# Last attention of a four-layer transformer kernel: VectorE takes over a quarter of GpSimd's subtractions of the row maximum

## The chip, the cores and the metric

One Trainium2 chip, one core. The metric is the device time of one execution in microseconds, as the median of several runs. The engines are named as in the profile: PE is TensorE (PEld its weight loads), DVE is VectorE, ACT is ScalarE, POOL is GpSimd, SP is SyncE, which issues DMAs.

## The reference, cut to what matters

Four layers, each an attention and a feed-forward block, on x of 16 sequences x 128 positions x 256 features. Everything is float32 unless a block quantizes. The change touches only the attention of the last layer:

```python
scores = jnp.einsum('bhqd,bhkd->bhqk', q, k) / np.sqrt(D)      # 32 heads of 8, keys of two windows
scores = scores + bias[None]                                   # ALiBi slopes
scores = jnp.where(mask[None, None], scores, -jnp.inf)         # 64 back for one half, 32 for the other
wei = jax.nn.softmax(scores, axis=-1)
return jnp.einsum('bhqk,bhkd->bhqd', wei, v)
```

## The kernel before, in words

The stage is `window_attention`. The work runs over 16 batches (one sequence of 128 positions each), written as pairs: `t` counts pairs and `j` is 0 or 1 in a pair. This text numbers the batches 0 to 15. Each batch has eight units (`U`), in two quads of four (`QUAD`). A unit is a 128 x 512 tile: four blocks of 128 rows (head and query) by 128 keys.

For each unit, four engines follow one another:

- PE computes the scores of a whole quad into four PSUM banks (`scores`, L3171). The first quad of a batch needs the queries spread by GpSimd (`made`) and the keys copied by ACT (`keyed`); each quad needs the four banks read by VectorE (`biased`).
- VectorE's `lower` (L3325): four instructions per unit add the table of slopes and mask to the scores, write the sum to `low` in SBUF and reduce the row maximum into `top`. One operand of each comes from PSUM, one from SBUF. The last of the four counts up `biased`.
- GpSimd's `lower` (L3141): one 128 x 512 instruction per unit subtracts `top` from `low` in place; both operands lie in SBUF. It counts up `lowered`.
- PE transposes the unit (`turn_probs`, L3180), ACT takes the exponential (L3274), and later PE multiplies by the values (`mix_up`, L3197).

GpSimd also spreads the queries of the next batch, in two instructions of 128 x 512 (`spread`, L2884). Its order in a batch is: lower of units 0 and 1, spread 0, lower of units 2 and 3, spread 1, lower of units 4 to 7.

VectorE's order in a batch is: `lower` of units 4 to 7; `normalize` of the second quad of the batch before (a reciprocal, L3336, and a product, L3338); `add` of the batch two back (x += result, L3344, and the statistics of the row, L3346); `lower` of units 0 to 3 of the next batch; `normalize` of this batch's first quad. Batch 1 has no `add` yet, batch 0 neither.

PE's order in a batch is written out by hand: transposes of units 0 and 1, scores of this batch's second quad, half of the batch before's product with the values, transpose of unit 2, `turn_mixed`, transpose of unit 3, `turn_back`, `go_down` (output projection of the batch two back), transposes of units 4 and 5, scores of the next batch's first quad, first half of this batch's product, transposes of units 6 and 7, `turn_back`. Each engine runs its queue in order, and a waiting instruction holds all that stands behind it.

Ahead of the last pair (batches 14 and 15) VectorE works out the variance of the first 12 row blocks (L2056 to L2061) and GpSimd its inverse root (`norm.root`, L2065), which stands on GpSimd's queue ahead of the subtractions of batch 14; `norm.shifts` (L2069) follows on VectorE in batch 15. SP moves values and results through HBM by DMA (`read_values`, `realign`), in step with `normalize`.

Of the kernel before, what the change touches and what calls it, by code (L numbers as in the profile page):

```python
# [9 lines left out]
ALU = mybir.AluOpType  # L10
# [4 lines left out]
P = 128  # L15
# [2864 lines left out]
def spread_queries(pool, w, c, queries, place):  # L2880

    query = queries.rearrange("p (i q) -> p i q", q=QB).unsqueeze(2).to_broadcast([P, NB, 4, QB])
    own = w.own[:, :].unsqueeze(1).unsqueeze(3).to_broadcast([P, NB, 4, QB])
    return pool.tensor_tensor(w.qd[:, place, :, c * (P // 2):(c + 1) * (P // 2)].rearrange("p i (m q) -> p i m q", q=QB), query, own, ALU.mult)  # L2884
# [186 lines left out]
def window_attention(nc, mem, norm):  # L3071


    U = NB
    QUAD = 4
    LOWS = 8
# [4 lines left out]
    with ctx:  # L3081
        def sb(what, shape, dt=F32):
            return ctx.enter_context(nc.sbuf_tensor(f"wa_{what}", shape, dt))
# [4 lines left out]
        def signal(what, per=1, credit=0):  # L3088
            return Signal(ctx, nc, f"wa_{what}", 2 * per, credit)
# [3 lines left out]
        low = mem.ctxt[:, :, :].rearrange("p c (l x n) -> p (c l) x n", l=LOWS // HC, x=QUAD)  # L3093
        pt = sb("pt", [P, U // 2, QUAD, 2, P])
        top = sb("top", [P, LOWS, QUAD])
# [13 lines left out]
        v_read = [Signal(ctx, nc, f"wa_v_read{j}", 32) for j in range(2)]  # L3109
        scored = signal("scored", U, 2 * U)  # L3110
        biased = signal("biased", U, 2)
        lowered = signal("lowered", U)
        turn = signal("turn", U, LOWS)
        pt_moved = signal("pt_moved", U, 2)
        mixed_s = signal("mixed", U // 2, U)
# [11 lines left out]
        with nc.Block() as block:  # L3127

            @block.gpsimd
            def _(pool):  # L3130
                pool.memset(v[:, :, :, WV:], 0.0).then_inc(padded.sem, 1)

                def spread(t, j, c):
                    if c == 0:
                        pool.wait_ge(scored.sem, scored.at(t, (j - 2) * U + U - 1))
                    spread_queries(pool, w, c, w.q[:, c, bass.ds((t * 2 + j) * S, S)], j % 2).then_inc(made.sem, 1)

                def lower(t, j, k):
                    pool.wait_ge(biased.sem, biased.at(t, j * U + k))
                    unit = low[:, k % LOWS, :, :]  # L3140
                    pool.tensor_tensor(unit, unit, top[:, k % LOWS, :].unsqueeze(2).to_broadcast([P, QUAD, P]), ALU.subtract).then_inc(lowered.sem, 1)  # L3141

                def batch(t, j, final=False):
                    for k in range(U):
                        lower(t, j, k)
                        if k in (1, 3) and not final:
                            spread(t, j + 1, k // 2)

                pool.sem_inc(made.sem, HC)
                for t in range(B // 2 - 1):  # L3150
                    batch(t, 0)
                    batch(t, 1)
                norm.root(pool, 0, 0, LASTG)
                batch(B // 2 - 1, 0)
                batch(B // 2 - 1, 1, final=True)

            @block.tensor
            def _(pe):
# [15 lines left out]
                                last.then_inc(scored.sem, 1)  # L3174

                def turn_probs(t, j, k):
                    pe.wait_ge(lowered.sem, lowered.at(t, j * U + k))
                    pe.wait_ge(pt_moved.sem, pt_moved.at(t, j * U + k - 2))
                    for x in range(QUAD):
                        last = pe.transpose(turned[k % 2][:, x * P:(x + 1) * P], low[:, k % LOWS, x, :], mem.ident[:, :])  # L3180
                    last.then_inc(turn.sem, 1)
# [68 lines left out]
                t = B // 2 - 1  # L3250
# [63 lines left out]
            @block.vector  # L3314
            def _(dve):
                for s in (biased, chain, added):
                    dve.sem_inc(s.sem, s.credit)

                def lower(t, j, k):
                    n = j * U + k  # L3320
                    unit = low[:, k % LOWS, :, :]
                    dve.wait_ge(scored.sem, scored.at(t, n))
                    dve.wait_ge(turn.sem, turn.at(t, n - LOWS))
                    for x in range(QUAD):
                        ins = dve.tensor_tensor_reduce(unit[:, x, :], score[k % QUAD][:, x * P:(x + 1) * P], w.table[:, k, x, :], 1.0, NEVER,  # L3325
                                                       ALU.add, ALU.max, top[:, k % LOWS, x:x + 1])
                    ins.then_inc(biased.sem, 1)

                def normalize(t, j, u):
                    def step(k, ins):  # L3330
                        ins.then_inc(chain.sem, 1)
                        dve.wait_ge(chain.sem, chain.at(t, 4 * j + 2 * u + k))

                    sums = back[:, :].rearrange("p (x k d) -> p x k d", x=QUAD, k=4)
                    dve.wait_ge(backed.sem, backed.at(t, 2 * j + u))
                    step(0, dve.reciprocal(inv[:, :, :], sums[:, :, :, WD]))  # L3336
                    dve.wait_ge(placed[u].sem, placed[u].at(t, 16 * j - 1))
                    step(1, dve.tensor_tensor(mixed[:, u, :, :].rearrange("p x (k d) -> p x k d", k=4), sums[:, :, :, 0:WD],  # L3338
                                              inv[:, :, :].unsqueeze(3).to_broadcast([P, QUAD, 4, WD]), ALU.mult))

                def add(t, j):
                    row = mem.x_tile(t * 2 + j)
                    dve.wait_ge(downed.sem, downed.at(t, j))
                    dve.tensor_tensor(row, row, od[:, H:2 * H], ALU.add).then_inc(added.sem, 1)  # L3344
                    dve.wait_ge(added.sem, added.at(t, j))
                    dve.bn_stats(mem.stats_tile(t * 2 + j), row).then_inc(stat.sem, 1)  # L3346

                def batch(t, j, before=2, final=False):
                    if final:
                        norm.shifts(dve, 0, 0, LASTG)  # L3350
                    for k in range(QUAD, U):
                        lower(t, j, k)
                    if before >= 1:
                        normalize(t, j - 1, 1)
                    if before >= 2:
                        add(t, j - 2)
                    if not final:
                        for k in range(QUAD):
                            lower(t, j + 1, k)
                    normalize(t, j, 0)  # L3360
                    if final:
                        norm.scales(dve, 0)
                        norm.lift(dve, 0)

                for k in range(QUAD):
                    lower(0, 0, k)
                batch(0, 0, before=0)
                batch(0, 1, before=1)
                for t in range(1, B // 2 - 1):
                    batch(t, 0)  # L3370
                    batch(t, 1)
                t = B // 2 - 1
                dve.wait_ge(stat.sem, stat.at(t, -3))
                norm.variance(dve, 0, LASTG)
                batch(t, 0)
                batch(t, 1, final=True)
                norm.round(dve, 0)
                normalize(t, 1, 1)
                add(t, 0)

# [420 lines left out]
def layer3_attention(nc, mem, A, norm):  # L3801
    ctx = Stage(nc)
    with ctx:
        def sb(name, shape, dt=F32):
            return ctx.enter_context(nc.sbuf_tensor(f"wa_{name}", shape, dt))

        w = mem.wa
        w.q = sb("q", [P, HC, T])
        w.kc, w.ko = sb("kc", [P, W_CTX + T]), sb("ko", [P, W_OWN + T])
        w.qd, w.keys = sb("qd", [P, 2, NB, P]), sb("keys", [P, 2, NB, P])  # L3810
        window_projections(nc, mem, mem.norm_projections)
        window_attention(nc, mem, norm)
# [273 lines left out]
```

## Time and profile before

| what | value |
|---|---|
| median of 3 runs | 2010.26 us (2015.07, 2008.82, 2010.26) |
| the profiled execution, its own time | 2015.13 us |
| its span, first to last instruction | 2013.4 us |
| mean granted TensorE clock | 0.963 of full speed |
| stage of the change, first scores to last statistics | 1703.5 to 1893.5 us of the span |

How to read it: the profiled execution is one run, 0.24% above the median; 1.7 us of it lie around the span. A timeline gives start and length in us, and in brackets the idle time of the engine before the instruction and what ended it; neighbours of one kind are merged, with their count behind an x. Pipelined instructions may overlap.

### The profile page before, as it was taken

What the parts mean: (1) busy time and instruction counts of PE and PEld (TensorE: products, weight loads), DVE (VectorE), ACT (ScalarE), POOL (GpSimd) and SP (SyncE); (2) the same over time, 40 slices, a digit from 0 to 9 for tenths busy, and PEclk for the clock granted to TensorE, in tenths of its full rate; (3) what the DMA queues carried; (4) which work ended last, traced back from release to release, by engine and by line L of the source; (5) the groups of instructions that cost most, each with busy time, mean ns of one, the idle gap of its engine ahead of it and who ended that gap; (6) DMA issues with size and microseconds to landing.
All of it is one profiled execution on the core that took longest, in us unless ns stands there. A gap on an engine that the chain in (4) does not pass through costs nothing. (4 is left out here: it accounts for less than half of the span.)

```text
span 2013.4 us, 42500 instructions
## 1 busy us (share of the span) xinstructions
PE 1792.1 (89%) x12207; PEld 1211.7 (60%) x12216; DVE 1264.2 (63%) x4137; ACT 1026.1 (51%) x2698; POOL 729.0 (36%) x707
## 2 busy tenths in 40 slices
PE   7999999998999888859899999987997879999765
PEld 4677777775555556645566666663554555787533
DVE  5666666664777534565543344446997954787697
ACT  5555555554333344411344444435887942666586
POOL 3333333332000100557455555552320011998420
PEclk9999999999999999979999999998998889999888
DMA  9990000000000000135577777650001021222100
GB/s 311 304 274 0 0 0 0 0 0 1 0 0 0 1 1 1 70 135 176 142 164 161 164 162 171 117 123 1 2 2 66 1 70 41 43 54 58 36 22 22
DMA packets 145607, 145.55 MB, mean 72 GB/s; under 512 B 49376, under 2 KB 133568, under 8 KB 145344
## 3 DMA queue, kind: packets, MB, share of 16 engines
q1 hardware_dynamic: 122432, 113.81, 19.5%
q0 software_dynamic: 23040, 30.01, 8.5%
q8 instruction: 75, 1.23, 0.3%
q14 instruction: 60, 0.49, 0.1%
HBM read 137.12 MB, written 66.44 MB: 101 GB/s over the span
## 5 line engine op out<-in xcount | busy, mean ns | idle before, releaser
L1709 POOL DMA_INDIRECT expert_sums<-moe_rows_in,moe_to x128 | 198.2, 1549 | 159.2 <-DMA expert_sums<-moe_rows_in,moe_to 101.6
L1782 PE MATMUL moe_gate<-moe_places,moe_xt 128*128 x512 | 175.9, 466 | 4.2 <-issue 2.0
L1975 DVE COPY moe_ht_e<-moe_turned 128x256 f32<-128x256 f32 x128 | 54.3, 424 | 194.4 <-PE moe_turned L1790 194.4
L570 ACT ACTIVATE ga_prob<-ga_score,ga_neg_max 128x128 f32<-128x128 f32 x256 | 99.6, 390 | 125.7 <-DVE ga_neg_max L443 125.7
L2065 POOL TENSOR_TENSOR ln_rstd<-ln_var,half 128x4 f32<-128x4 f32 (+1 forms) x16 | 21.4, 1338 | 367.2 <-DVE ln_var L2061 367.2
L190 POOL TENSOR_TENSOR ga_q_inv<-ga_q_sum,half 128x4 f32<-128x4 f32 x64 | 64.4, 1007 | 224.4 <-DVE ga_q_sum L426 224.4
L3325 DVE CUSTOM_DVE_ANT_0 ctxt<-wa_score,early 128x128 f32<-128x128 f32 x512 | 110.8, 287 | 46.9 <-PE wa_score L3171 46.9
L3141 POOL TENSOR_TENSOR ctxt<-ctxt,wa_top 128x512 f32<-128x512 f32 x128 | 129.8, 1040 | 17.1 <-DVE wa_top L3325 17.1
L325 PE MATMUL ga_summed<-ga_wo,ga_out_t 128*128 128x256 f32 x512 | 121.2, 380 | 0.7 <-ACT ga_out_t L578 0.7
L1782 PEld LDWEIGHTS moe_gate<-moe_places,moe_xt 128*128 128x128 f32 x512 | 90.8, 190 | 48.6 <-issue 13.6
L249 PE MATMUL ga_proj<-early,ga_xt 128*128 128x512 f32 x252 | 119.8, 598 | 0.0
L1116 POOL DMA_INDIRECT slot_x<-early x96 | 98.6, 1027 | 54.1 <-issue 27.1
L439 DVE SCALAR_TENSOR_TENSOR ga_score<-ga_scored,ga_q_inv,ga_mask 128x128 f32<-128x128 f32 x256 | 72.2, 344 | 51.6 <-PE ga_scored L297 51.2
L325 PEld LDWEIGHTS ga_summed<-ga_wo,ga_out_t 128*128 128x128 f32 x512 | 92.3, 190 | 11.0 <-ACT ga_out_t L578 1.1
L1889 ACT ACTIVATE moe_act_e<-moe_gate 128x176 f32<-128x176 f32 x128 | 40.6, 317 | 101.6 <-PE moe_gate L1782 101.6
L3180 PE MATMUL wa_turned<-ident,ctxt 128*128 128x128 f32 x512 | 77.3, 286 | 11.3 <-POOL ctxt L3141 10.0
L3274 ACT ACTIVATE wa_pt<-wa_turned 128x512 f32<-128x512 f32 x128 | 73.1, 596 | 25.8 <-PE wa_turned L3180 23.3
L431 DVE COPY ga_qt<-ga_turned 128x512 f32<-128x512 f32 x63 | 43.4, 689 | 62.6 <-PE ga_turned L289 62.5
L297 PEld LDWEIGHTS ga_scored<-ga_kt,ga_qt 128*128 128x128 f32 x512 | 63.7, 192 | 23.6 <-DVE ga_qt L431 13.9
L556 ACT ACTIVATE ga_square<-ga_q_tok 128x128 f32<-128x128 f32 x256 | 75.0, 294 | 1.5 <-DVE ga_q_tok L394 1.4
L297 PE MATMUL ga_scored<-ga_kt,ga_qt 128*128 128x128 f32 x512 | 72.5, 285 | 0.9 <-DVE ga_qt L431 0.9
L1884 ACT ACTIVATE moe_xt<-moe_up 128x256 f32<-128x256 f32 x128 | 49.2, 384 | 47.0 <-PE moe_up L1771 36.5
(491 smaller groups left out, 4700.2 us busy)
## 6 DMA issues: line engine op xcount, KB each, us to landing
moe_places<-in_L_ffn_packed SPq DMA_DIRECT2D x128, 608.0 KB
slot_x<-zeros SPq DMA_DIRECT2D x24, 1076.0 KB, 14.8
moe_rows_in<-slot_x SPq DMA_DIRECT2D x128, 134.5 KB, 3.2
wa_v<-v_ctx SPq DMA_DIRECT2D x16, 180.0 KB, 3.2
early<-in_L_xattn_Wq SPq DMA_DIRECT2D x5, 512.0 KB, 7.8
x<-in_x SPq DMA_DIRECT2D x4, 512.0 KB, 9.6
ga_wo<-in_L_xattn_Wo SPq DMA_DIRECT2D x1, 2048.0 KB, 15.0
expert_sums<-zeros SPq DMA_DIRECT2D x2, 1024.0 KB, 7.9
```

The costliest lines, as they stand in the source:

```text
L249: last = pe.matmul(proj[m % 2][:, :], lhs[:, c, :], weight[:, c, :], start=(c == 0), stop=(c == HC - 1))
L297: last = pe.matmul(scored[n % 2][:, h * P:(h + 1) * P], qt[:, n % 2, h * P:(h + 1) * P], kt[:, b % 2, g, :], start=True, stop=True)
L325: last = pe.matmul(summed[:, 0:H], out_t[:, h, :], w.wo[:, h, :], start=(h == 0), stop=(h == NH - 1))
L556: last = act.activation(square[:, h, :], q_tok[:, n % 2, h * D:(h + 1) * D], ACT.Square, accum_out=q_sum[:, n % 2, h:h + 1])
L570: last = act.activation(prob[:, n % 2, part], score[:, n % 2, part], ACT.Exp, bias=neg_max[:, n % 2, h:h + 1], accum_out=total[:, n % 2, h ...
L1116: pool.indirect_dma_start(out=self.mem.slot_x, out_offset=bass.IndirectOffsetOnAxis(ap=self.slot_to[:, t, k:k + 1], axis=0), in_=self.mem. ...
L1709: pool.indirect_dma_start(out=mem.sums[j % SUMS], out_offset=bass.IndirectOffsetOnAxis(ap=to[:, j:j + 1], axis=0), in_=y[:, j, :], in_offs ...
L1782: last = pe.matmul(both[j % 2][:, 0:2 * FE], xt[:, j % 2, c, :], packed[:, place, c * 2 * FE:(c + 1) * 2 * FE].rearrange("p a n -> p (a n) ...
L3141: pool.tensor_tensor(unit, unit, top[:, k % LOWS, :].unsqueeze(2).to_broadcast([P, QUAD, P]), ALU.subtract).then_inc(lowered.sem, 1)
L3180: last = pe.transpose(turned[k % 2][:, x * P:(x + 1) * P], low[:, k % LOWS, x, :], mem.ident[:, :])
L3274: act.activation(pt[:, k // 2, :, k % 2, :], turned[k % 2][:, :].rearrange("p (x m) -> p x m", x=QUAD), ACT.Exp).then_inc(pt_moved.sem, 1)
L3325: ins = dve.tensor_tensor_reduce(unit[:, x, :], score[k % QUAD][:, x * P:(x + 1) * P], w.table[:, k, x, :], 1.0, NEVER, ALU.add, ALU.max, ...
```

## The change

VectorE subtracts the maximum of units 3 and 7 itself, after `lower` of the quad that they end, and waits for its own `biased` first; a semaphore `lowered_v` tells PE. GpSimd subtracts for units 0, 1, 2, 4, 5, 6. The second spread is tied to unit 2 and no longer to unit 3.

```diff
-        lowered = signal("lowered", U)
+        lowered = signal("lowered", U - 2)
+        lowered_v = signal("lowered_v", 2)
...
                 def batch(t, j, final=False):
                     for k in range(U):
-                        lower(t, j, k)
-                        if k in (1, 3) and not final:
-                            spread(t, j + 1, k // 2)
+                        if k % QUAD < QUAD - 1:
+                            lower(t, j, k)
+                        if k in (1, 2) and not final:
+                            spread(t, j + 1, k - 1)
...
                 def turn_probs(t, j, k):
-                    pe.wait_ge(lowered.sem, lowered.at(t, j * U + k))
+                    u, r = divmod(k, QUAD)
+                    if r == QUAD - 1:
+                        pe.wait_ge(lowered_v.sem, lowered_v.at(t, j * 2 + u))
+                    else:
+                        pe.wait_ge(lowered.sem, lowered.at(t, j * (U - 2) + u * (QUAD - 1) + r))
...
+                def subtract(t, j, u):
+                    k = QUAD * u + QUAD - 1
+                    unit = low[:, k % LOWS, :, :]
+                    dve.wait_ge(biased.sem, biased.at(t, j * U + k))
+                    dve.tensor_tensor(unit, unit, top[:, k % LOWS, :].unsqueeze(2).to_broadcast([P, QUAD, P]), ALU.subtract).then_inc(lowered_v.sem, 1)
...
                     for k in range(QUAD, U):
                         lower(t, j, k)
+                    subtract(t, j, 1)
                     if before >= 1:
                         normalize(t, j - 1, 1)
...
                         for k in range(QUAD):
                             lower(t, j + 1, k)
+                        subtract(t, j + 1, 0)
                     normalize(t, j, 0)
...
                 for k in range(QUAD):
                     lower(0, 0, k)
+                subtract(0, 0, 0)
```

## Rows read from the trace of the kernel before

**Rows 1.** The page, busy time, share of the span and instructions of each engine.
```profile
PE 1792.1 (89%) x12207; PEld 1211.7 (60%) x12216; DVE 1264.2 (63%) x4137; ACT 1026.1 (51%) x2698; POOL 729.0 (36%) x707
```

**Rows 2.** Stretches between the first scores of consecutive batches: busy time of each engine.
```profile
core 0: us, PE busy (x) PEld busy (x) DVE busy (x) ACT busy (x) POOL busy (x), PEclk, DMA share, GB/s
1725.54:1736.50 10.96, 10.55 (x239) 9.03 (x238) 8.52 (x70) 6.96 (x13) 10.01 (x11) 1.00 0.26 54
...
1845.22:1856.10 10.88, 10.56 (x240) 9.04 (x239) 8.71 (x71) 7.11 (x14) 10.03 (x11) 1.00 0.26 54
1856.10:1874.27 18.17, 12.17 (x239) 10.37 (x238) 9.47 (x77) 7.06 (x14) 13.36 (x13) 0.81 0.16 33
```

**Rows 3.** Waits from 1735 to 1873 us: total, times, longest (us).
```profile
PEld wa_turned L3180 <- POOL ctxt L3141: 9.6, 12, 6.0
```

**Rows 4.** Timeline of GpSimd in one batch.
```profile
1771.34 2.04 POOL L3141 TENSOR_TENSOR ctxt<-ctxt,wa_top 128x512 f32<-128x512 f32 x2 [0.85 <-DVE wa_top L3325]
1773.33 1.04 POOL L2884 TENSOR_TENSOR wa_qd<-wa_q,early 128x512 f32<-128x512 f32 x1
...
1777.33 4.04 POOL L3141 TENSOR_TENSOR ctxt<-ctxt,wa_top 128x512 f32<-128x512 f32 x4
```

**Rows 5.** Timeline of PE in the same batch.
```profile
1771.27 1.09 PE L3180 MATMUL wa_turned<-ident,ctxt 128*128 128x128 f32 x8
...
1774.02 1.17 PE L3171 MATMUL wa_score<-wa_keys,wa_qd 32*128 32x128 f32 x32
...
1779.01 1.06 PE L3180 MATMUL wa_turned<-ident,ctxt 128*128 128x128 f32 x8
1780.01 1.17 PE L3171 MATMUL wa_score<-wa_keys,wa_qd 32*128 32x128 f32 x32
```

**Rows 6.** Timeline of VectorE around the same batch's first half.
```profile
1767.81 0.26 DVE L3336 RECIPROCAL wa_inv<-wa_back 128x16 f32<-128x16 f32 x1
...
1768.42 0.42 DVE L3344 TENSOR_TENSOR x<-x,wa_mix_t 128x256 f32<-128x256 f32 x1
1768.88 0.43 DVE L3346 BATCH_NORM_STATS2 stats<-x 128x6 f32<-128x256 f32 x1
...
1770.33 0.29 DVE L3325 CUSTOM_DVE_ANT_0 ctxt<-wa_score,early 128x128 f32<-128x128 f32 x1 [1.02 <-PE wa_score L3171]
...
1773.71 0.25 DVE L3336 RECIPROCAL wa_inv<-wa_back 128x16 f32<-128x16 f32 x1
...
1775.30 0.29 DVE L3325 CUSTOM_DVE_ANT_0 ctxt<-wa_score,early 128x128 f32<-128x128 f32 x1 [1.02 <-PE wa_score L3171]
```

**Rows 7.** By line: instructions of these kinds, ns min/median/max.
```profile
L420 DVE TENSOR_TENSOR ga_k_rms<-ga_k_tok,ga_k_inv x16: 681/692/694, 17.0 to 450.1; 128x512 f32<-128x512 f32 x16
...
L3141 POOL TENSOR_TENSOR ctxt<-ctxt,wa_top x128: 1036/1040/1046, 1705.7 to 1884.5; 128x512 f32<-128x512 f32 x128
```

**Rows 8.** Timeline and lines: VectorE and GpSimd, both with two SBUF operands, side by side.
```profile
L2069 DVE SCALAR_TENSOR_TENSOR ln_shift<-ln_mean,ln_rstd x16: 150/158/1074, 452.1 to 1929.1; 128x4 f32<-128x4 f32 x12, 128x12 f32<-128x12 f32 x4
...
1876.48 4.04 POOL L3141 TENSOR_TENSOR ctxt<-ctxt,wa_top 128x512 f32<-128x512 f32 x4 [1.91 <-DVE wa_top L3325]
...
1879.47 1.07 DVE L2069 SCALAR_TENSOR_TENSOR ln_shift<-ln_mean,ln_rstd 128x12 f32<-128x12 f32 x1
...
1880.46 0.28 DVE L3325 CUSTOM_DVE_ANT_0 ctxt<-wa_score,early 128x128 f32<-128x128 f32 x1
...
L2010 DVE TENSOR_TENSOR x<-x,moe_places x8: 406/420/772, 1345.2 to 1360.5; 128x256 f32<-128x256 f32 x8
...
L1718 POOL TENSOR_TENSOR x<-x,moe_places x8: 715/722/904, 1345.3 to 1358.2; 128x256 f32<-128x256 f32 x8
...
1349.54 1.58 POOL L1718 TENSOR_TENSOR x<-x,moe_places 128x256 f32<-128x256 f32 x2
...
1349.77 0.77 DVE L2010 TENSOR_TENSOR x<-x,moe_places 128x256 f32<-128x256 f32 x1
```

**Rows 9.** Timeline ahead of batch 14: VectorE's end of its lowers, GpSimd's inverse root.
```profile
1860.67 0.26 DVE L3336 RECIPROCAL wa_inv<-wa_back 128x16 f32<-128x16 f32 x1
...
1862.21 2.27 POOL L2065 TENSOR_TENSOR ln_rstd<-ln_var,half 128x12 f32<-128x12 f32 x1 [4.76 <-DVE ln_var L2061]
```

## The prediction

> **What bounds the kernel now.** The page comes first and settles little: PE is busy for 89% of the span, GpSimd for 36% [rows 1], but that averages many stages. So the stage is cut into batches. Twelve stretches, from the first scores of batch 2 to those of batch 14, last 10.87 us each within 0.1, and in each PE is busy for 10.55, GpSimd for 10.0, VectorE for 8.7 [rows 2] (the first and the last of the twelve stand there). Two engines are close to full, and which of them sets the 10.87 has to be read from order and waits, not from shares.
>
> Take VectorE's first `lower` of a batch as zero, D = 1770.33 [rows 6]. GpSimd starts 1.01 later (1771.34) and then issues one instruction per 1.00 us: units 0 and 1, spread 0 (1773.33, D+3.00), and so on, until unit 7 ends at 1777.33 + 4.04 = 1781.37 [rows 4]. PE transposes units 0 and 1 as GpSimd yields them and issues the second quad's scores at 1774.02, D+3.69. From there to the next batch's scores (1780.01, D+9.68) its own list of work fills the time. The test is units 4 and 5, the last subtractions ahead of those scores: their eight transposes take 1.06 us, and those of units 6 and 7, whose subtractions lay ready long before, take 1.09 [rows 5]. So GpSimd delays PE at units 4 and 5 by nothing that shows; it arrives just in time. PE's weight loads do wait for GpSimd, 9.6 us in 12 waits, but 6.0 of that is one wait ahead of batch 14 [rows 3], and what remains, about 0.33 per batch, belongs to units 0 and 1, which the change leaves as they are. VectorE has slack in two places: 1.02 us ahead of each quad's first `lower` [rows 6].
>
> **What the change removes.** Two GpSimd instructions of 1.04 us [rows 7] per batch, 32 in all. Only unit 3 stands ahead of units 4 and 5, which come about 1 us earlier; PE doesn't wait for them, so this is worth 0. Units 0 and 1 follow VectorE, not GpSimd's backlog: GpSimd idles 0.85 ahead of unit 0 already [rows 4]. The cover that makes the removal worthless is PE's own list. Tying the second spread to unit 2 moves nothing: GpSimd's order is units 0, 1, spread 0, unit 2, spread 1, unit 4 either way, once unit 3 is gone.
>
> **What it adds.** Two VectorE subtractions per batch of 128 x 512 with both operands in SBUF. The nearest row of the same kind and size lasts 0.69 us (L420) [rows 7]. If that were all, each would fit into a 1.02 us slack, with the wait on its own `biased` (about 0.11: an estimate for the last accumulator read and the semaphore; between add and statistics such a wait shows 0.04, 1768.84 to 1768.88 [rows 6]). Behind the first subtraction stand `normalize` and the second quad's lowers; behind the second stand `normalize`, `add` and the next batch's lowers, so what overflows the slack reaches D.
>
> **What the two engines do to each other.** In this stage an instruction of 0.158 us on VectorE with two SBUF operands lasted 1.07: it began at 1879.47 and ended at 1880.54, 0.02 behind GpSimd's run of subtractions (1876.48 + 4.04 = 1880.52) [rows 8]. Elsewhere VectorE's sum of 0.42 came upon a GpSimd sum of 0.72 begun at 1349.54 (to 1350.26), and ended at 1350.54: 0.28 behind it, 0.14 short of its full length; the second GpSimd sum then ended at 1351.12, 0.58 behind VectorE, again 0.14 short [rows 8]. So the later one waits out the earlier and keeps a lead of about 0.13, and VectorE gets in between two GpSimd instructions. VectorE's `lower` reads PSUM and escapes: sixteen took 3.38 us beside a busy GpSimd (1770.33 to 1773.71) [rows 6].
>
> Walk through one batch after the change:
> - First subtraction ready at D + 3.38 + 0.11 = D+3.49. GpSimd is in spread 0, from D+3.01 to D+4.05. It ends at F = D + 4.05 + 0.69 - 0.13 = D+4.61.
> - GpSimd's unit 2 ends at F + 1.04 - 0.14 = F+0.90. Unit 4 starts at F+1.86, unit 5 at F+2.86, unit 6 at F+3.86, and that ends at F+4.90.
> - VectorE's next instruction begins 0.08 ahead of the end (1880.46 against 1880.54 [rows 8]); `normalize` takes 0.61 (1767.81 to 1768.42 [rows 6]). Unit 4's `lower` starts at F+0.53, and the second subtraction is ready at F + 0.53 + 3.49 = F+4.02.
> - That is 0.16 behind the start of GpSimd's unit 6. It waits and ends at F + 4.90 + 0.56 = F+5.46.
> - Then `normalize` 0.61, `add` 0.46 (1768.42 to 1768.88), statistics 0.43 less 0.08 [rows 6]: the next D is F + 5.46 - 0.08 + 0.61 + 0.46 + 0.35 = F+6.80 = D+11.41.
>
> PE would allow D+10.87. VectorE becomes the bound, by **0.54 us per batch**. Batches 2 to 13 carry the whole list: 12 x 0.54 = 6.5. Batch 1 has no `add` (0.8 less) and fits. PE's transposes of units 3 and 7 then wait for F and F+5.46; PE comes to them later than that.
>
> Ahead of batch 14 the first subtraction stands between the last `lower` (1860.67) and the variance, behind which GpSimd has idled 4.76 us [rows 9], and PE 6.0 [rows 3]. GpSimd being idle, it costs 0.69 + 0.11 - 0.08 = 0.72, all on the path. In batches 14 and 15 the second subtraction ends ahead of PE's scores or of the tail, so nothing is added. SP's value loads and stores follow `normalize` by some 0.7 to 1.8 us more and have several us of room: 0.
>
> **Sum**: 6.5 + 0.7 = 7.2 us. The profiled execution of 2015.13 would become 2022.3; it lies 0.24% above the median of 2010.26, which becomes **2017.5**.
>
> The Trainium skill, "SBUF — State Buffer", section "Who interferes with whom", says that a VectorE instruction with two SBUF inputs and a GpSimd instruction that reads SBUF exclude each other, and that the second to issue "fully blocks" until the first has ended. The rows agree on the exclusion and differ on the full block, by the lead of 0.13. By the page, F would be D+4.74, the next D F+7.07, the excess 0.94 per batch, and the time 2022.3, with the second subtraction a mere 0.03 behind unit 6.
>
> **The rivals.**
> - *The second subtraction slips ahead of GpSimd's unit 6.* It then ends at F + 3.90 + 0.56 = F+4.46, the next D would be F+5.80 = D+10.41, below PE's 10.87, and only the 0.7 ahead of batch 14 is left: 2011.0, no change. It decides if the subtraction is ready 0.16 us earlier against GpSimd than worked out. For it: the margin is thin, and every term has an error of some hundredths. Against it: at 1879.47 VectorE still lost to a GpSimd instruction of the run that began within hundredths of it [rows 8]. The same time results if a subtraction with a broadcast operand escapes the exclusion. Chance 0.27.
> - *VectorE doesn't get in between GpSimd's instructions and waits until GpSimd idles.* Then F = D + 6.05 + 0.56 = D+6.61, unit 4's `lower` starts at D+7.14, GpSimd's units 4 to 6 end at D+11.20, and the next D is D+13.10: 2.2 x 12 + 0.7, 2037.5. Against it stand the two GpSimd sums at 1349.54 with VectorE's between them [rows 8]. Chance 0.05.
> - *The full block of the page*, 2022.3: 0.04.
> - *GpSimd was the bound after all* and loses an instruction of 1.00 per batch on its loop from unit 0 to unit 5: 13 fewer, 1998. Against it is the 1.06 beside 1.09 [rows 5]. Chance 0.04.
>
> **How the numbers follow.** The forecast above has 0.60; its own range is 2014.5 to 2020.5 (0.54 moves with the subtraction's length by twice 0.07, the runs scatter by several us). Within 0.3% (6.0 us) is about what a measurement of this kernel can't tell from no change. Of the forecast, 0.48 lies above that and 0.12 below. Slower: 0.48 + 0.05 + 0.04 = 0.57. Same: 0.12 + 0.27 = 0.39. Faster: 0.04. The range runs from 2009 (no change, with scatter) to 2022.5 (the full block).
>
> **What would show it.** Stretches between first scores of 11.4 us, with PE's busy time unchanged. VectorE's subtractions of about 1.1 us (the first, ending 0.56 behind spread 0) and 1.4 us (the second, 0.56 behind unit 6), not 0.69; GpSimd's unit 2 about 0.46 longer. No wait of VectorE for scores ahead of a batch, and PE's weight loads waiting more for GpSimd's unit 0. GpSimd's inverse root 0.7 later against the last `lower` of batch 14. Wrong would be: stretches of 10.9 with a second subtraction of 0.7 to 1.0 us (it slipped ahead), or of 9.9 (GpSimd was the bound).

## The result: slower, by the steps forecast, and at a time outside the range

The changed kernel ran 2027.36 us as the median of four runs (2018.74 to 2031.82), the kernel before 2009.65 (the three runs listed above and a fourth, 2009.04); the ratio is 1.0077, interval 1.0045 to 1.0109. The direction was forecast; the time lies 9.9 us above the forecast of 2017.5 and 4.9 above the top of the range. Measured again, twice, with 12 runs of the changed kernel beside 35 of the one before, the ratio is 1.0027 (1.0004 to 1.0051) and 1.0032 (1.0007 to 1.0057), against the forecast 2017.5 / 2010.26 = 1.0036.

The profiled execution after took 2018.74 us (span 2016.9). The page's row of engines, to lay beside [rows 1]:

```profile
PE 1787.8 (89%) x12207; PEld 1212.4 (60%) x12216; DVE 1298.4 (64%) x4169; ACT 1026.5 (51%) x2698; POOL 704.0 (35%) x675
```

VectorE has 32 instructions more, GpSimd 32 fewer. VectorE's sum grew by 34.2 us, where 32 x 0.69 would be 22.1. The stretches from first scores to first scores, one that stands for eleven equal ones and the one ahead of batch 15 (columns as in [rows 2]):

```profile
1764.82:1776.17 11.35, 10.60 (x240) 9.09 (x239) 11.11 (x73) 7.12 (x14) 8.48 (x8) 1.00 0.25 51
1855.62:1875.65 20.03, 12.87 (x240) 10.92 (x239) 12.09 (x82) 7.10 (x14) 10.30 (x9) 0.83 0.14 30
```

10.87 has become 11.35. PE is as busy as before (10.60 beside 10.55), at the same granted clock of 1.00; VectorE is now busy for 11.11 of the 11.35, GpSimd for 8.48 where it was 10.0.

One batch after the change, GpSimd first, then VectorE (its lowers left out but for the first of each quad), then PE:

```profile
1767.52 2.04 POOL L3142 TENSOR_TENSOR ctxt<-ctxt,wa_top 128x512 f32<-128x512 f32 x2 [2.87 <-DVE wa_top L3331]
1769.52 1.04 POOL L2884 TENSOR_TENSOR wa_qd<-wa_q,early 128x512 f32<-128x512 f32 x1
1770.52 1.49 POOL L3142 TENSOR_TENSOR ctxt<-ctxt,wa_top 128x512 f32<-128x512 f32 x1
1771.97 1.04 POOL L2884 TENSOR_TENSOR wa_qd<-wa_q,early 128x512 f32<-128x512 f32 x1
1772.97 3.04 POOL L3142 TENSOR_TENSOR ctxt<-ctxt,wa_top 128x512 f32<-128x512 f32 x3
```

```profile
1765.73 0.42 DVE L3356 TENSOR_TENSOR x<-x,wa_mix_t 128x256 f32<-128x256 f32 x1
1766.19 0.43 DVE L3358 BATCH_NORM_STATS2 stats<-x 128x6 f32<-128x256 f32 x1
1766.53 0.27 DVE L3331 CUSTOM_DVE_ANT_0 ctxt<-wa_score,early 128x128 f32<-128x128 f32 x1
...
1770.02 1.09 DVE L3339 TENSOR_TENSOR ctxt<-ctxt,wa_top 128x512 f32<-128x512 f32 x1
...
1771.64 0.29 DVE L3331 CUSTOM_DVE_ANT_0 ctxt<-wa_score,early 128x128 f32<-128x128 f32 x1
...
1775.14 1.41 DVE L3339 TENSOR_TENSOR ctxt<-ctxt,wa_top 128x512 f32<-128x512 f32 x1
...
1777.88 0.28 DVE L3331 CUSTOM_DVE_ANT_0 ctxt<-wa_score,early 128x128 f32<-128x128 f32 x1
```

```profile
1764.82 1.17 PE L3173 MATMUL wa_score<-wa_keys,wa_qd 32*128 32x128 f32 x32
1766.37 1.10 PE L3203 MATMUL wa_mix_t<-wa_pt,wa_v 128*32 128x64 f32 x64 [0.37 <-issue]
```

The walk of the prediction can be laid over these rows, with D = 1766.53:

| step | forecast | measured |
|---|---|---|
| first subtraction ready | D+3.49 | 1770.02, D+3.49 |
| its length, its end F | 1.1 us, D+4.61 | 1.09, 1771.11, D+4.58 |
| GpSimd's unit 2 ends | F+0.90 | 1770.52 + 1.49 = 1772.01, F+0.90 |
| GpSimd's unit 6 ends | F+4.90 | 1772.97 + 3.04 = 1776.01, F+4.90 |
| second subtraction ready | F+4.02 | 1775.14, F+4.03 |
| its length, its end | 1.4 us, F+5.46 | 1.41, 1776.55, F+5.44 |
| next D | F+6.80, D+11.41 | 1777.88, F+6.77, D+11.35 |

No wait is left between VectorE's instructions: the 1.02 us ahead of each quad [rows 6] are gone, and its list sets the batch. PE shows it as 0.37 us of idle time ahead of its product (L3203). The profile names no releaser for it ("issue"), but in the code the product waits for `added` of the batch two back, and the `add` above ended at 1765.73 + 0.42 = 1766.15, 0.22 before the product.

Then the two ends. Ahead of batch 14 (VectorE, then GpSimd), beside [rows 9]:

```profile
1860.82 0.69 DVE L3339 TENSOR_TENSOR ctxt<-ctxt,wa_top 128x512 f32<-128x512 f32 x1
1861.42 0.25 DVE L3348 RECIPROCAL wa_inv<-wa_back 128x16 f32<-128x16 f32 x1
```

```profile
1862.96 2.27 POOL L2065 TENSOR_TENSOR ln_rstd<-ln_var,half 128x12 f32<-128x12 f32 x1 [7.50 <-DVE ln_var L2061]
```

Here GpSimd is idle, and the same subtraction takes 0.69. In batch 15 (VectorE, then PE):

```profile
1885.84 1.10 DVE L3339 TENSOR_TENSOR ctxt<-ctxt,wa_top 128x512 f32<-128x512 f32 x1
1886.86 0.24 DVE L3348 RECIPROCAL wa_inv<-wa_back 128x16 f32<-128x16 f32 x1
1887.14 0.29 DVE L3350 TENSOR_TENSOR tail_mixed<-wa_back,wa_inv 128x128 f32<-128x128 f32 x1
1887.47 0.42 DVE L3356 TENSOR_TENSOR x<-x,wa_mix_t 128x256 f32<-128x256 f32 x1
```

```profile
1885.67 1.04 PE L3186 MATMUL wa_turned<-ident,ctxt 128*128 128x128 f32 x8
1888.10 1.10 PE L3203 MATMUL wa_mix_t<-wa_pt,wa_v 128*32 128x64 f32 x64 [1.40 <-ACT wa_pt L3280]
```

PE stood for 1.40 us ahead of the product of batch 15. The profile names ScalarE's exponential, but the last exponentials that this product needs are those of units 1 and 3; the `add` of batch 13 ended at 1887.89, 0.21 before the product, the same distance as in the batch above. In the kernel before, the same product follows without a wait, but its `add` had ended only 0.28 us ahead of it (1884.57 + 0.42 = 1884.99), and had itself waited for PE's output projection:

```profile
1884.57 0.42 DVE L3344 TENSOR_TENSOR x<-x,wa_mix_t 128x256 f32<-128x256 f32 x1 [0.15 <-PE wa_mix_t L3218]
```

```profile
1885.26 1.10 PE L3197 MATMUL wa_mix_t<-wa_pt,wa_v 128*32 128x64 f32 x64
```

So in batch 15 there was next to no room for a later `add` before either.

The stage, cut into the same pieces in every kernel (us from first scores to first scores; "within 14" is from first to second scores of batch 14, "last" from the second scores of batch 15 to the start of the last statistics, and "stage" ends there too, 0.43 ahead of the 1893.5 that the table of the kernel before has for their end). The first stretch is 11.11, 11.30 or 12.03 in executions of one and the same kernel, and is longer where the granted clock is lower, so it is none of the change; here batch 0 of before and of after, the clock in the third column from the end:

```profile
1703.57:1714.66 11.09, 8.14 (x88) 6.47 (x88) 6.94 (x64) 3.82 (x7) 8.70 (x9) 0.69 0.47 102
```

```profile
1697.33:1709.35 12.02, 9.35 (x88) 7.42 (x88) 8.22 (x66) 3.57 (x7) 8.16 (x8) 0.58 0.43 95
```

| kernel | batch 0 | batch 1 | mean of 2 to 13 | within 14 | last | stage |
|---|---|---|---|---|---|---|
| before | 11.11 | 10.88 | 10.88 | 11.48 | 13.92 | 189.5 |
| after | 12.03 | 10.33 | 11.33 | 12.71 | 15.38 | 198.6 |
| after, again | 11.11 | 10.32 | 11.32 | 12.71 | 15.49 | 197.1 |
| after, third time | 11.30 | 10.33 | 11.33 | 12.71 | 15.38 | 197.0 |
| reduction in place of subtraction | 11.11 | 9.93 | 10.85 | 12.20 | 14.66 | 189.7 |
| unit 3 alone | 12.03 | 10.32 | 10.86 | 12.21 | 14.00 | 190.7 |
| unit 7 alone | 12.03 | 10.88 | 10.97 | 11.51 | 14.77 | 193.5 |
| unit 7 behind the statistics | 12.03 | 10.32 | 10.85 | 12.21 | 14.26 | 191.0 |
| units 3 and 7 not subtracted | 12.04 | 9.93 | 10.91 | 11.49 | 13.92 | 190.4 |
| unit 7 behind the statistics in batch 15 only | 11.13 | 10.33 | 11.32 | 12.70 | 14.26 | 195.9 |
| before, late inverse root | 12.03 | 10.88 | 10.88 | 4.88 | 14.97 | 185.8 |
| before, late root and late shift | 11.11 | 10.88 | 10.88 | 4.88 | 14.22 | 184.1 |

### The profile page after: what moved, and what is told of

It reads as the page before. It is cut to its first block and busy times, and to the rows that moved or that the text cites. A ratio compares the mean times of both kernels' runs of the same rounds, so it can differ in the third digit from the quotient of the medians.

```text
span 2016.9 us, 42500 instructions
## 1 busy us (share of the span) xinstructions
PE 1787.8 (89%) x12207; PEld 1212.4 (60%) x12216; DVE 1298.4 (64%) x4169; ACT 1026.5 (51%) x2698; POOL 704.0 (35%) x675
## 5 line engine op out<-in xcount | busy, mean ns | idle before, releaser
L3142 POOL TENSOR_TENSOR ctxt<-ctxt,wa_top 128x512 f32<-128x512 f32 x96 | 104.1, 1105 | 47.1 <-DVE wa_top L3331 47.1
L3186 PEld LDWEIGHTS wa_turned<-ident,ctxt 128*128 128x128 f32 x512 | 58.1, 145 | 23.6 <-POOL ctxt L3142 17.1
```

## The experiments

The intervals of most of these ratios overlap, and that of the changed kernel (1.0027, from 1.0004 to 1.0051) too. So it is the stretches and lengths of one profiled execution of each kernel that decide between the theories, not the times.

**The changed kernel once more.** No edit.

> The changed kernel once more, unaltered, to see where the runs some 9 to 13 us above the profiled one (2018.7 against 2027 to 2032) lose their time. Theory 1 (the exclusion alone): the stage is 9 us longer than before in every run (stretches of 11.35 us instead of 10.87), the rest is scatter of other stages, and the median comes out near 2009.6 + 9 = 2018 to 2020. Theory 2 (something else in this stage comes on top in most runs, such as a lower granted clock because PE now idles in each batch): the median stays at 2025 to 2029, and a profile of such a run shows a granted clock of 0.5 inside the stage or stretches above 11.4 us.

Measured: 2019.19 us (2010.13 to 2027.93, 12 runs), the kernel before beside it 2013.39 (2004.18 to 2026.64, 35 runs), ratio 1.0027 (1.0004 to 1.0051). Against the table's first row the stage is 7.6 us longer (the 9 us expected came from the first profile, where batch 0 alone took 0.9 more): -0.6 in batch 1, +5.3 in batches 2 to 13 (scores to scores), +1.2 within batch 14, +1.6 at the end.

**A reduction in place of each subtraction.** VectorE runs as many instructions, of the same 128 x 512, in the same places, but each reads one operand from SBUF; the maximum of units 3 and 7 stays in.

```diff
-                    dve.tensor_tensor(unit, unit, top[:, k % LOWS, :].unsqueeze(2).to_broadcast([P, QUAD, P]), ALU.subtract).then_inc(lowered_v.sem, 1)
+                    dve.tensor_reduce(spare[:, :], unit, AX.X, ALU.max).then_inc(lowered_v.sem, 1)
```

> VectorE's two subtractions per batch are replaced by a reduction of the same 128 x 512 tile that reads one operand from SBUF and writes a spare column; the maximum of units 3 and 7 is left in. Same work of about 0.69 us on VectorE, same waits, GpSimd relieved as in the change. Theory 1 (two SBUF operands exclude GpSimd): the reductions take 0.69 us beside GpSimd, the stretches are 10.85 to 10.90 us, only the 0.7 to 1.2 us ahead of batch 14 is left: 2010 to 2012. Rival (VectorE simply has 1.4 us of work too much per batch): stretches stay at 11.3 us and the time near the changed kernel's.

Measured: 2010.38 us, ratio 0.9993 (0.9971 to 1.0015). One line of the trace decides it (least, median and greatest length in ns), with the subtractions of the changed kernel under it:

```profile
L3340 DVE TENSOR_REDUCE wa_spare<-ctxt x32: 685/686/687, 1706.2 to 1881.5; 128x4 f32<-128x512 f32 x32
```

```profile
L3339 DVE TENSOR_TENSOR ctxt<-ctxt,wa_top x32: 692/1099/1416, 1702.9 to 1885.8; 128x512 f32<-128x512 f32 x32
```

With one operand in SBUF all 32 take 0.69 beside the same GpSimd list, and the batch is back at 10.85. VectorE does not simply have too much to do; it is held up. The reduction also writes less (128 x 4 beside 128 x 512). That it is not the writing that escapes is shown by `lower` in the kernel before: it writes its blocks of 128 x 128 to SBUF, with one operand in SBUF, and none of the 512 lasted longer than 0.293 us.

```profile
L3325 DVE CUSTOM_DVE_ANT_0 ctxt<-wa_score,early x512: 279/286/293, 1704.7 to 1883.6; 128x128 f32<-128x128 f32 x171
```

**One subtraction alone.** Unit 3 by VectorE and unit 7 by GpSimd, and the other way round:

```diff
-                    subtract(t, j, 1)
```

```diff
-                        subtract(t, j + 1, 0)
...
-                subtract(0, 0, 0)
```

(GpSimd and PE's waits follow; with unit 7 alone the spreads are as before.)

> VectorE subtracts for unit 3 alone, GpSimd for the other seven. Theory 1: the subtraction still waits for spread 0 (about 1.1 us long), but unit 4's lowers start only about 0.2 us late and the rest of VectorE's list ends at D+9.95, below PE's 10.87: stretches of 10.87, plus 0.7 to 1.2 ahead of batch 14, 2010 to 2012. Rival (each waiting subtraction costs its share of the loss): half of the 0.48 us per batch, stretches of 11.1 us.

> VectorE subtracts for unit 7 alone, GpSimd for the other seven. Theory 1: the subtraction is ready at D+8.46, waits for GpSimd's unit 5 and ends at D+9.6; the next D is D+10.94, 0.07 above PE's 10.87: stretches of 10.87 to 10.95, nothing ahead of batch 14, 2009.6 to 2011. Rival (each waiting subtraction costs its share): stretches of 11.1 us, some 3 us more than before.

Measured: 2015.79 us, ratio 1.0009 (0.9989 to 1.0029), and 2017.72, 1.0019 (0.9995 to 1.0043). Both times lie above those expected, which were reckoned from 2009.65 where the kernel before now had 2013.39.

```profile
L3338 DVE TENSOR_TENSOR ctxt<-ctxt,wa_top x16: 691/1095/1099, 1708.1 to 1879.0; 128x512 f32<-128x512 f32 x16
```

```profile
L3338 DVE TENSOR_TENSOR ctxt<-ctxt,wa_top x16: 945/1110/1119, 1722.9 to 1894.5; 128x512 f32<-128x512 f32 x16
```

Each is held up by about 0.4 us also when it is alone (the first of the two is unit 3's, the second unit 7's), and the batch still takes 10.86 or 10.90 (the mean of 10.97 has three longer stretches in it): a block of that size fits into VectorE's slack. Only both together exceed it. What each costs at the ends separates too: unit 3 adds 12.21 - 11.48 = 0.73 within batch 14, unit 7 adds 14.77 - 13.92 = 0.85 at the end.

**The second subtraction moved, not removed.**

```diff
-                    subtract(t, j, 1)
                     if before >= 1:
                         normalize(t, j - 1, 1)
                     if before >= 2:
                         add(t, j - 2)
+                    subtract(t, j, 1)
```

> The second subtraction (unit 7) moves behind `normalize`, `add` and the statistics, just ahead of the next batch's `lower`; the first stays. Number of instructions and operands as in the changed kernel. Theory 1 (it is the two blocks by GpSimd that make VectorE the bound): by the forecast's walk the second subtraction is then ready at D+9.9, where GpSimd's unit 6 has ended (D+9.5); it lasts 0.69 us and not 1.4, the next D could be D+10.55, below PE's 10.87. Period 10.85 to 10.87 us, stage 190 to 192 us, time within 0.15% of the kernel before. Rival (VectorE has too much work, or the order behind a wait counts wherever it stands): period 11.2 to 11.4, stage 196 to 198.

Measured: 2017.98 us beside 2018.33, ratio 0.9998 (0.9980 to 1.0017). The same instructions, the second two places later, where GpSimd's run is over. First all 32 (their middle lies between the two kinds), then a second one of a batch:

```profile
L3339 DVE TENSOR_TENSOR ctxt<-ctxt,wa_top x32: 672/1004/1100, 1706.4 to 1884.1; 128x512 f32<-128x512 f32 x32
```

```profile
1777.74 0.67 DVE L3339 TENSOR_TENSOR ctxt<-ctxt,wa_top 128x512 f32<-128x512 f32 x1
```

None takes 1.41 any more: from batch 2 on the second lasts 0.67 to 0.68, the first still 1.09 to 1.10 (0.69 ahead of batch 14), and the batch is at 10.85. What is left of the change's cost is 0.7 within batch 14 and 0.3 at the end.

**GpSimd's relief alone.** Neither engine subtracts the maximum of units 3 and 7 (that part is left out); PE waits for `biased` there.

```diff
-                        pe.wait_ge(lowered_v.sem, lowered_v.at(t, j * 2 + u))
+                        pe.wait_ge(biased.sem, biased.at(t, j * U + k))
...
-                    subtract(t, j, 1)
...
-                        subtract(t, j + 1, 0)
...
-                subtract(0, 0, 0)
```

> Units 3 and 7 are not lowered by their maximum at all (this part of the computation is left out): GpSimd is relieved of two instructions per batch, VectorE gets none, PE waits for `biased` there. Theory 1: PE's own list sets the batch, so the relief is worth 0: period 10.85 to 10.87, stage 188 to 189.5, as before. Rival (GpSimd was the bound and its relief was eaten up by VectorE's additions): period 9.9 to 10.3, stage 176 to 182, time 0.4 to 0.6% below before.

Measured: 2019.60 us beside 2018.33, ratio 0.9997 (0.9974 to 1.0020). A stretch of it:

```profile
1763.36:1774.21 10.85, 10.53 (x242) 9.06 (x246) 8.71 (x71) 7.10 (x15) 8.03 (x8) 1.00 0.26 54
```

GpSimd is busy for 8.0 us instead of 10.0 and the batch is 0.02 shorter (ten of the twelve stretches; one is 11.58, which with a batch 0 of 12.04 puts the stage above the 189.5 expected). GpSimd was not the bound there. In batch 1, where PE has no output projection yet, it was: that one stretch fell from 10.88 to 9.93, here and with the reductions, and to 10.32 with unit 3's relief and VectorE's own subtraction of it, but not at all with unit 7's.

**The end of the last batch.** The changed kernel, with unit 7 subtracted behind `add` in batch 15 only.

```diff
-                    subtract(t, j, 1)
+                    if not final:
+                        subtract(t, j, 1)
...
                         add(t, j - 2)
+                    if final:
+                        subtract(t, j, 1)
```

> The changed kernel, in the last batch alone with VectorE's second subtraction behind `add` and its statistics. Theory (the 1.5 us that the end of the last batch grew by is PE's product of batch 15 waiting for VectorE's `add` of batch 13, which stands behind that subtraction): from the second scores of batch 15 to the last statistics 14.0 to 14.5 us, against 15.4 to 15.5 in the changed kernel and 13.9 before; the period of batches 3 to 14 stays 11.35. Rival (unit 7's transpose and exponential are what comes late): 15.2 us or more.

Measured, one run: the period stays 11.32, and the end falls from 15.4 to 14.26. The 0.3 us that are left against 13.92 were not followed up.

```profile
1883.66 0.42 DVE L3356 TENSOR_TENSOR x<-x,wa_mix_t 128x256 f32<-128x256 f32 x1
1884.11 0.43 DVE L3358 BATCH_NORM_STATS2 stats<-x 128x6 f32<-128x256 f32 x1
1884.45 0.68 DVE L3339 TENSOR_TENSOR ctxt<-ctxt,wa_top 128x512 f32<-128x512 f32 x1
```

```profile
1884.29 1.10 PE L3203 MATMUL wa_mix_t<-wa_pt,wa_v 128*32 128x64 f32 x64 [0.27 <-ACT wa_pt L3280]
```

The `add` ends at 1884.08, the product starts 0.21 later. With an earlier `add` PE's wait fell from 1.40 to 0.27, so it was for the `add`, whatever the profile called it.

**A version that beats both.** The one large wait in the profile of before was never part of the change: GpSimd's inverse root holds its queue for 4.76 us ahead of batch 14 [rows 9], and PE with it for 6.0 [rows 3]. The kernel before, with the root two units into batch 15:

```diff
+                        if k == 1 and final:
+                            norm.root(pool, 0, 0, LASTG)
...
-                norm.root(pool, 0, 0, LASTG)
                 batch(B // 2 - 1, 0)
```

> The kernel before, with one line moved: GpSimd's inverse root no longer stands ahead of its subtractions of batch 14 but behind unit 1 of batch 15, ahead of `norm.shifts` still. Theory 1 (the 6.0 us wait of PE ahead of batch 14 is GpSimd's queue held by the root's wait for the variance): the stretch from the first scores of batch 14 to its second, 11.5 us before, falls to 4.9 to 6.0, the stage from 189.5 to 182.5 to 185, the time by 0.25 to 0.35%. Rival (the wait only moves to `norm.shifts` and so to VectorE's second quad of batch 15): stretch of batch 14 as above, but first to second scores and on to the last statistics 2 to 5 us longer; stage 186 to 190, time the same.

Measured: 2012.17 us (2004.67 to 2016.65) beside 2018.33, ratio 0.9962 (0.9947 to 0.9978). The stretch that took 18.17 us at a granted clock of 0.81 [rows 2]:

```profile
1858.63:1871.03 12.40, 10.96 (x242) 8.95 (x243) 11.21 (x75) 7.22 (x15) 10.06 (x11) 1.00 0.23 48
```

The wait is gone, and with it the low clock behind it: PE is busy for 10.96 instead of 12.17. The stretch is 5.77 us shorter: PE's busy time in it fell by 1.21 and its idle time by 4.56 of 6.00, since PE now waits 0.78 and 0.34 us there for GpSimd's subtractions of units 4 and 5. The stage of 185.8 lies just above the 182.5 to 185 of theory 1; its batch 0 took 12.03. The rival had a part in it: VectorE waits for the root ahead of the shift, and the end grew by 14.97 - 13.92 = 1.05.

```profile
1877.50 0.92 DVE L2069 SCALAR_TENSOR_TENSOR ln_shift<-ln_mean,ln_rstd 128x12 f32<-128x12 f32 x1 [1.42 <-POOL ln_rstd L2065]
```

So the shift was moved too:

```diff
-                    if final:
-                        norm.shifts(dve, 0, 0, LASTG)
                     for k in range(QUAD, U):
                         lower(t, j, k)
+                        if final and k == QUAD:
+                            norm.shifts(dve, 0, 0, LASTG)
```

> As the kernel with the late inverse root, and `norm.shifts` behind VectorE's `lower` of unit 4 of batch 15 instead of ahead of it. In the run before VectorE waited 1.42 us there for the root, and the shift itself lasted 0.92. Theory: unit 5's `lower` starts some 0.8 us earlier, and from the second scores of batch 15 to the last statistics it takes 14.0 to 14.4 us instead of 14.97; the time 0.3 to 0.45% below the kernel before. Rival (ScalarE's normalizations then come too late and hold its exponentials): 15 us or more.

Measured: 2007.96 us (2001.48 to 2017.70) beside 2013.67, ratio 0.9970 (0.9953 to 0.9986); the end is 14.22 and the stage 184.1, 5.4 us below before. Between the two versions themselves the times do not tell, and of the 1.7 us between their stages 0.9 is batch 0 (12.03 and 11.11); the end, 14.97 and 14.22, does.

**The changed kernel a third time.**

> The changed kernel once more, unchanged, to settle how much of its first time belongs to the change. If the change costs what the stage shows (7.6 to 9.1 us longer) and the rest was scatter outside the stage: stage 196.5 to 199, period 11.3 to 11.35, ratio to the kernel before 1.002 to 1.006. If the first measurement (2027, 0.77% above) was the change's own: ratio 1.006 to 1.010, with first scores of the stage later than in the kernel before, run beside run.

Measured: 2023.51 us (2016.46 to 2038.39, 12 runs) beside 2018.33 (2010.59 to 2028.59, 35 runs), ratio 1.0032 (1.0007 to 1.0057), stage 197.0. The upper value 1.0057 shuts out the first ratio of 1.0077, though not its interval.

The two profiles of this kernel that came of the second and the third measurement, on different chips, differ by 16.9 us of span, and the difference is there before the stage begins. First, span and mean granted clock of the one and the other; then a line of the MoE stage, which the change does not touch (its first start is 1345.2 in the kernel before [rows 8]), first in the second measurement:

```profile
core 0: 2008.3 us, clock 0.968
```

```profile
L2010 DVE TENSOR_TENSOR x<-x,moe_places x8: 407/422/495, 1335.1 to 1350.9; 128x256 f32<-128x256 f32 x8
```

and in the third:

```profile
core 0: 2025.2 us, clock 0.960
```

```profile
L2010 DVE TENSOR_TENSOR x<-x,moe_places x8: 406/414/491, 1351.9 to 1367.1; 128x256 f32<-128x256 f32 x8
```

1335.1 against 1351.9: 16.8 us, in the same instructions. It is not the chip alone: on the chip of the second measurement the kernel with unit 7 alone, whose code differs in the last attention only, reached them at 1353.1.

```profile
L2010 DVE TENSOR_TENSOR x<-x,moe_places x8: 407/416/492, 1353.1 to 1368.4; 128x256 f32<-128x256 f32 x8
```

One place where such time arises is the feed-forward block at 490 us: the same groups of four instructions in the kernel before and after.

```profile
492.68 2.92 PE L694 MATMUL sf_gate<-sf_wg,sf_xt 128*128 128x512 f32 x4 [0.47 <-ACT sf_xt L756]
...
504.04 3.54 PE L694 MATMUL sf_gate<-sf_wg,sf_xt 128*128 128x512 f32 x4 [2.31 <-ACT sf_xt L756]
```

```profile
491.03 1.98 PE L694 MATMUL sf_gate<-sf_wg,sf_xt 128*128 128x512 f32 x4 [0.47 <-ACT sf_xt L756]
...
500.70 1.96 PE L694 MATMUL sf_gate<-sf_wg,sf_xt 128*128 128x512 f32 x4 [2.31 <-ACT sf_xt L756]
```

Behind the same short waits the granted clock was lower in one execution and not in the other; the windows of these groups, before and after:

```profile
492.68:495.40 2.72, 2.72 (x5) 1.16 (x5) 0.16 (x1) 1.72 (x2) 0.41 (x1) 0.67 0.00 0
504.04:507.42 3.38, 3.38 (x4) 1.48 (x5) 3.38 (x9) 0.25 (x1) 0.00 (x0) 0.53 0.02 5
```

```profile
491.03:492.85 1.82, 1.82 (x4) 0.87 (x5) 0.16 (x1) 1.72 (x2) 0.42 (x1) 1.00 0.00 0
500.70:502.49 1.79, 1.79 (x5) 0.83 (x5) 1.79 (x4) 0.24 (x1) 0.00 (x0) 1.00 0.03 9
```

## Why the prediction was right, and where it failed

**The mechanism held, step by step.** PE's own list set the 10.87 in batches 2 to 13: the relief of GpSimd alone gives 10.85. The added subtraction and GpSimd's instructions exclude each other: 1.09 and 1.41 us where the forecast had 1.1 and 1.4; it lasts 0.69 with GpSimd idle, and so does a reduction with one operand in SBUF beside a busy GpSimd. It takes both: each alone, or the second one moved to where GpSimd has finished, leaves the typical batch at 10.85 to 10.90. The next D came at D+11.35 against D+11.41. The subtraction ahead of batch 14 costs 0.73 where 0.72 was forecast.

**The rivals.** The second subtraction did not slip ahead of unit 6 (1.41 us long). VectorE did get in between GpSimd's instructions (1771.11, ahead of unit 2's end). That GpSimd was the bound is false for batches 2 to 13 and true for batch 1, one stretch of 0.95 us that the prediction had not looked at. The full block would have given D+11.81; the measured batch is 11.35. The Trainium skill, "SBUF — State Buffer", section "Who interferes with whom", says too that a VectorE instruction with at most one SBUF input, outside the 2-port modes, does not contend with GpSimd: the reductions at 0.686 agree. On the block the trace goes on differing from that page: the first subtraction ended 1771.11 - 1770.56 = 0.55 behind the end of the spread, not 0.69. (The words "fully blocks" stand there for the 2-port modes; of two SBUF inputs the section says "contends", under its rule of "an exclusive lock".)

**Terms of the sum.** Three were off, and that they nearly cancel is luck. Forecast by D's, 12 x 0.54 = 6.5; measured between scores 5.3, plus 0.5 by which VectorE's first `lower` lags the scores at the end (1857.33 - 1855.62 = 1.71, before 1.19), together 5.9. Not in the sum: -0.6 in batch 1. Wrong in the sum: "In batches 14 and 15 the second subtraction ends ahead of PE's scores or of the tail, so nothing is added." It named the wrong consumer. What stands behind the second subtraction is `add`, and PE's product waits for that by `added`; in batch 15, where PE has no next scores to do first, the end grew by 1.5 us, and 1.1 of that goes when the subtraction stands behind the statistics there. The stage grew by 7.5 to 7.6 us where its first stretch ran alike, against a sum of 7.2.

**What failed is the term for everything else**: "the runs scatter by several us", read from three runs that lay within 6.3 us, and a median of 2010.26 taken for the kernel's level; the top of the range, 2022.5, was the full block with no scatter on it at all. 87 more runs of the kernel before lay between 2004.18 and 2028.59. They come from three comparisons on three chips, with medians of 2013.39, 2018.33 and 2013.67. Each chip was used at one time only, so what the chip and what the hour did cannot be told apart. On which chip the first measurement ran is not known, and three of its four runs of the kernel before were the old ones. The changed kernel's own medians moved along with those beside them, 2019.19 and 2023.51: the first lies inside the forecast's own range, the second again above the whole range. The first four runs, at 2018.74 to 2031.82, lie inside what it did later (2010.13 to 2038.39).

So the price of the change, some 0.3%, was forecast. The first measurement holds some 10 us more, 2027.36 - 2009.65 = 17.7 beside the 7.5 of the stage. No trace shows where its three runs at 2027 to 2032 spent them; the like run of the third measurement, at 2027.02, has a stage of 197.0, and was late before the stage began. The range should have carried a shift of the whole level by 8 us or more beside the bounds of the stage. Over the 83 runs of the comparison with the median of 2013.39, a fit with one slope for all five kernels and a level for each gives about 1 us less per 0.001 more of mean granted clock, with 3.6 us left over; the first four runs had 0.957 to 0.964, so the clock goes with a part of it. What sets it from run to run, and the rest, was not found: that stays open.

## What to carry to other kernels

Before an operation moves from a busy engine to a less busy one, lay the two engines' lists of one period side by side in time: an instruction that excludes the other engine's costs its length plus what is left of the other's, less about 0.13 us here, and it is the place in the list that decides (1.41 us, and 0.67 two places later). Then go through every semaphore that the instructions behind it raise, not only its own, in the last iteration as well, where the work that hid a wait is missing. And take the scatter of the level from more than three runs, or forecast the ratio to a kernel run beside it, on the same chip.

## What was not expected of the hardware

- Two executions reach the same instruction of a stage that the change does not touch 16.8 us apart on two chips (1335.1 and 1351.9, at mean granted clocks of 0.968 and 0.960), and 18.0 us apart on one chip (1335.1 and 1353.1, at 0.968 and 0.957); identical groups of four matmuls took 1.98 us at a granted clock of 1.00 or 2.92 at 0.67, and 1.96 or 3.54 at 0.53, behind waits of the same length.
- Taking away a wait of PE of some 6 us took the low clock behind it away too: the stretch ran at a granted clock of 1.00 where it had 0.81 before, and PE's busy time in it fell from 12.17 to 10.96 us. The stretch itself became shorter by 5.77 us, since PE found another wait in it.
- The name that the profile gives to a releaser can be wrong: 1.40 us "for" an exponential was a wait for an addition that ended 0.21 us before the product, and still 0.21 before it in the run where the addition came earlier and the wait was 0.27.
